# Attention and expert kernel on one core: the order of SyncE's queue at a change of batch

## Chip, cores and metric

The kernel runs on one core of a Trainium2 chip. The metric is the device time of one execution in microseconds (us), smaller is better. A time of the kernel before is the median of three runs.

## The reference, cut to what matters

`x` is 8 x 1024 x 256 (batch, tokens, model), all in float32. A layer norm gives `xn`; attention (16 heads of 64, causal) and a mixture of experts (8 experts, the best 2 of each token, hidden size 1024) both read `xn`, and both are added to `x`:

```python
x = L0_attn_x
xn = _layernorm(x, axis=-1)
# attention
qkv = jnp.einsum('bse,ehd->bshd', xn, w_qkv)
q, k, v = jnp.split(qkv, 3, axis=-1)
out = _attention(q, k, v)                 # causal softmax
a = jnp.einsum('bshd,hde->bse', out, w_out)
# experts: gate[..., None] * y[topi, pos_c], summed over the two choices
x = x + a + _L0_ffn_ref(xn, wg, w1, b1, w2, b2)
```

## The kernel before, in words

Four stages follow one another: layer norm and router, the assignment of tokens to experts, the experts (their results go to `y` in HBM), and then `attention_and_sum`, the longest, in which everything here lies. It computes attention and, beside it, fetches each token's two expert rows and adds them.

**Units.** The attention stage has 64 units: 8 batches (`BATCH`) x 8 pairs of heads (`PAIRS`). Unit `n` belongs to batch `n // 8`, pair `n % 8`. A unit has 20 steps in five rounds of four; each engine walks through the same list of (unit, step), with its own list of what it does at which step. The 1024 queries of a unit are 8 rows of 128, and two rows make a group, 0 to 3. **Group 2 (rows 4 and 5) is the third group, group 3 (rows 6 and 7) the fourth.**

**The probabilities' path.** TensorE computes scores (L1231), VectorE the row minimum (L1355), ScalarE the exponential (L1293), GpSimd scales (L1436). The scaled probabilities must be transposed before TensorE can multiply them by the values (L1263). Groups 0 and 1 are transposed by TensorE. For groups 2 and 3 VectorE transposes 32 x 32 squares (L1398, into `squares`), and then 16 DMAs per group bring each strip of squares to its place in `pT`: 12 of them issued by SyncE in `place` (L1079 to L1085), 4 by GpSimd in `place_rest` (L1460 to L1465). The values product of group 2 of unit `n` runs at step 7 of unit `n + 1`, that of group 3 at step 15 of unit `n + 1`; each waits until all 16 of its strips have landed.

**The result rows.** `res` (128 x 8 x 256 float32, 1 MB, a single buffer) holds the rows of one batch in four groups of 256 KB. It starts as `x` (loaded by `refill`, L1091 to L1094); VectorE adds each pair's output projection to group `g` (L1381, piece `o0` to `o3`), GpSimd adds a tile of expert rows once per unit (`total`, L1500). After the last pair of a batch a group is written out (`store`, L1087 to L1089) and then loaded with the next batch's `x` (`refill` waits for the landing of that group's store, L1093). For unit `n` the pieces `o0` to `o3` belong to unit `n - 1`. So at a change of batch (`n` = 8, 16, ..., 56: seven of them) `store(b-1, 0)` to `store(b-1, 2)` become possible in the middle of unit `n` (VectorE steps 6, 10, 12), but `store(b-1, 3)` only at step 2 of unit `n + 1`. The next batch's `res` is first needed by `total(n)` (GpSimd, step 4 of unit `n + 1`, group 0) and by `o0` to `o3` of unit `n + 1` (VectorE, steps 6, 10, 12 and step 2 of the unit after).

**SyncE's queue** is written out by hand (L1099 to L1125). It is in order: where an instruction waits, all behind it wait. Per unit: the weights `wr` for unit `n + 2` (`load_w`, L1073, two DMAs, once GpSimd has finished with the buffer), one tile of `xn` (L1110), `place(n - 1, 3)`, at a change of batch stores and refills, `place(n, 2)`, and in every second unit the value weights `wvr` (`load_wv`, L1077, two DMAs, once GpSimd is done with the old ones). Before the change, at a change of batch, stores and refills of groups 0 to 2 stand between `place(n - 1, 3)` and `place(n, 2)`, and store and refill of group 3 at the end of the unit, behind `load_wv`. Next in the queue come `load_w`, the `xn` tile and `place(n, 3)` of the following turn of the loop:

```python
if n > 0:
    place(n - 1, 3)
if b > 0 and u == 0:
    for g in range(3):
        store(b - 1, g)
    for g in range(3):
        refill(b, g)
if n < UNITS - 1:
    place(n, 2)
if n % 2 == 0 and n // 2 + 2 < UNITS // 2:
    e.wait_ge(wvlo.sem, wvlo.at(n // 2, MC))
    load_wv(n // 2 + 2)
if b > 0 and u == 0:
    store(b - 1, 3)
    refill(b, 3)
```

Of the kernel before, what the change touches and what calls it, by code (L numbers as in the profile page):

```python
# [845 lines left out]
def attention_and_sum(nc, k, x, xn_dram, w_qkv, w_out, pick, y_dram, out, start):  # L846
# [7 lines left out]
    GROUPS = SEQ // GQ  # L854
# [77 lines left out]
    class Pieces:  # L932
        def __init__(self, sem_, own):
            self.sem, self.value, at = sem_, {}, 0
            for n in range(-1, UNITS + 1):
                for _, p in pieces(n):
                    at += own(p)
                    self.value[n, p] = at
# [5 lines left out]
    with ExitStack() as c:  # L944
# [45 lines left out]
        with ExitStack() as pre:  # L990
# [7 lines left out]
            @block.sync  # L998
            def _(e):
                e.dma_start(wo_raw, wov).then_inc(s_wo, 16)  # L1000
# [63 lines left out]
        def strip(g, a, b):  # L1064

            to, of = slice(b * BL, (b + 1) * BL), slice(a * BL, (a + 1) * BL)
            return wide[g][to, a].rearrange("p x r -> p (x r)"), sq[g][of, b].rearrange("p x k i -> p (x k i)")

        @block.sync
        def _(e):  # L1070
            def load_w(m):
                for c_ in range(MC):
                    e.dma_start(wr[:, 2 * c_:2 * c_ + 2], wv[m % PAIRS][:, c_, :, 0:2 * HDIM]).then_inc(wload.sem, 16)  # L1073

            def load_wv(m):
                for c_ in range(MC):
                    e.dma_start(wvr[:, c_], wvv[m % (PAIRS // 2)][:, c_, :, 2 * HDIM:]).then_inc(wvload.sem, 16)  # L1077

            def place(n, g):  # L1079
                e.wait_ge(squared.sem, squared.at(n, 4 * g - 4))  # L1080
                if n > 0:
                    e.wait_ge(pv.sem, pv.at(n - 1, RUN_OF[g] + 1))
                for a in range(QUARTERS - 1):
                    for b in range(QUARTERS):
                        e.dma_start(*strip(g, a, b)).then_inc(placed[g].sem, 16)  # L1085

            def store(b, g):  # L1087
                e.wait_ge(dve.sem, dve.at((b + 1) * PAIRS, f"o{g}"))
                e.dma_start(outv[:, b, 2 * g:2 * g + 2], res[:, 2 * g:2 * g + 2]).then_inc(stored[g].sem, 16)  # L1089

            def refill(b, g):  # L1091
                if b > 0:
                    e.wait_ge(stored[g].sem, stored[g].at(b - 1, 16))  # L1093
                e.dma_start(res[:, 2 * g:2 * g + 2], xv[:, b, 2 * g:2 * g + 2]).then_inc(rload[g].sem, 16)  # L1094

            e.dma_start(xnt[:], xnv[AHEAD]).then_inc(xload.sem, 16)
            load_w(1)
            load_wv(1)
            for n in range(UNITS):  # L1099
                b, u = n // PAIRS, n % PAIRS  # L1100
                if n == 0:
                    e.wait_ge(s_wolo, 1)
                    for g in range(GROUPS):
                        refill(0, g)
                if n + 2 < UNITS:
                    e.wait_ge(wlo.sem, wlo.at(n, MC))
                    load_w(n + 2)
                if n + 1 + AHEAD < TILES:
                    e.wait_ge(filled.sem, filled.at(n, "xn"))
                    e.dma_start(xnt[:], xnv[n + 1 + AHEAD]).then_inc(xload.sem, 16)  # L1110
                if n > 0:
                    place(n - 1, 3)
                if b > 0 and u == 0:
                    for g in range(3):
                        store(b - 1, g)
                    for g in range(3):
                        refill(b, g)
                if n < UNITS - 1:
                    place(n, 2)
                if n % 2 == 0 and n // 2 + 2 < UNITS // 2:  # L1120
                    e.wait_ge(wvlo.sem, wvlo.at(n // 2, MC))
                    load_wv(n // 2 + 2)
                if b > 0 and u == 0:
                    store(b - 1, 3)
                    refill(b, 3)  # L1125
            for g in range(GROUPS):
                store(BATCH - 1, g)
            for g in range(GROUPS):
                e.wait_ge(stored[g].sem, stored[g].at(BATCH - 1, 16))

        @block.tensor
        def _(e):
# [47 lines left out]
            def turn_p(n, name):  # L1180
                W, unit, at = work_bank(name), min(n, UNITS - 1), 0
                i, h, _, _ = TURNS[name][-1]
                e.wait_ge(scaled.sem, scaled.at(unit, SCALE_ORDER.index((i, h)) + 1))
                for i, h, k0, blocks in TURNS[name]:
                    for b in range(blocks):
                        cols = slice(OFFSET[i] + (k0 + b) * P, OFFSET[i] + (k0 + b + 1) * P)
                        ins = e.transpose(W[:, at * P:(at + 1) * P], room_of(unit, i, h)[:, cols], k["ident"][:])  # L1187
                        at += 1
                return ins

            def work(n, name):

                same = [(m, p) for m in (n - 1, n) if m >= -1 for _, p in pieces(m) if BANK_OF.get(p, 0) == BANK_OF[name]]
                same = same[:same.index((n, name))]
                if same:
                    m, p = same[-1]
                    if by_act(p):
                        e.wait_ge(act.sem, act.at(m, p))
                    if by_dve(p):
                        e.wait_ge(dve.sem, dve.at(m, p))  # L1200
                if name[0] == "p":
                    ins = project(n, name)
                elif name[0] == "v":
                    ins = values_of(n, name)
                elif name == "xn":
                    ins = turn_xn(n)
                elif name[0] == "t":
                    ins = turn_p(n, name)
                else:
                    ins = out_project(n, name)  # L1210
                ins.then_inc(filled.sem, 1)
# [359 lines left out]
```

## Time and profile before

| | |
|---|---|
| median of three runs | 2915.8 us (2915.28 to 2918.36) |
| the profiled execution, its own time | 2915.7 us |
| its span, first to last instruction | 2913.9 us |
| TensorE busy | 2814.5 us, 97% |
| VectorE / ScalarE / GpSimd busy | 2084.7 / 1699.7 / 1723.0 us |
| mean granted TensorE clock | 0.988 |
| mean DMA rate | 128 GB/s; about 150 GB/s in the attention stage |

The profile is of one execution. Its times count from the first instruction; the execution's own time is 1.8 us longer than the span. PE is TensorE, DVE VectorE, ACT ScalarE, POOL GpSimd, SP or SPq SyncE's queue of DMA issues. A line number such as L1085 is that of the kernel's listing. "pT<-squares" is a DMA or a product that writes `pT` from `squares`.

### The profile page before, as it was taken

The numbers are of one execution on the slowest core, as the hardware profiler recorded it, in microseconds if no ns is written. First come the engines' busy times: TensorE is split into PE (matmuls) and PEld (weight loads), VectorE is DVE, ScalarE is ACT, GpSimd is POOL, SyncE is SP. The second block draws the span as 40 slices with busy tenths as digits, with TensorE's granted clock in tenths as the row PEclk, the third lists the DMA queues.
The fourth block names the chain that finished last, engine by engine and source line by source line (L and its number), as shares of the span: only waits on it lengthen the run. The fifth ranks groups of instructions, "written<-read, shape, count | busy, mean of one in ns | idle before, by whom it ended". The sixth has DMA issues, their size and how long they took to land.

```text
span 2913.9 us, 61264 instructions
## 1 busy us (share of the span) xinstructions
PE 2814.5 (97%) x21321; PEld 2284.1 (78%) x21321; DVE 2084.7 (72%) x4448; ACT 1699.7 (58%) x3934; POOL 1723.0 (59%) x2631
## 2 busy tenths in 40 slices
PE   5599999999998999999999999999999999999998
PEld 4489999899997777777777777777777777777776
DVE  7843444344434888888888888888888888888886
ACT  3454444445454666666666666666666666666664
POOL 3032122211212777777877877777777778777774
PEclk9799999999999999999999999999999999999999
DMA  7022212221212565665665565665665556556553
GB/s 241 29 82 75 69 52 83 76 68 47 82 54 74 141 158 144 163 154 145 168 150 145 147 170 147 157 166 142 157 164 151 149 146 176 141 145 183 136 134 93
DMA packets 248774, 371.58 MB, mean 128 GB/s; under 512 B 77392, under 2 KB 177744, under 8 KB 248480
## 3 DMA queue, kind: packets, MB, share of 16 engines
q1 hardware_dynamic: 216000, 276.31, 35.3%
q0 software_dynamic: 32480, 91.44, 11.7%
q8 instruction: 174, 2.85, 0.4%
q14 instruction: 120, 0.98, 0.1%
HBM read 102.80 MB, written 33.55 MB: 47 GB/s over the span
## 4 chain that ended last, share of the span: by engine, by line
PE 66%; DVE 1%; SPq 1%; DMA 0%; issue 0%; ACT 0%; POOL 0%; DVEq 0%; ACTq 0%
PE O L1263 18%; PE S L1231 16%; PE W L1142 12%; PE W L1157 7%; PE W L1176 7%; PE W L1187 6%; SPq L1085 1%; DVE pr L1355 0%; PE W L1165 0%; DMA pT<-squares 0%; DVE squares L1398 0%; ACT pr L1293 0%; DMA out<-res 0%; ACT pT L1283 0%; DVE res L1381 0%
## 5 line engine op out<-in xcount | busy, mean ns | idle before, releaser
L1436 POOL TENSOR_SCALAR pr<-pr,rinv 128x512 f32<-128x512 f32 (+7 forms) x1024 | 748.4, 744 | 399.7 <-DVE rinv L1361 398.6
L1293 ACT ACTIVATE pr<-pr,negm 128x512 f32<-128x512 f32 (+7 forms) x1024 | 787.3, 774 | 285.3 <-DVE negm L1355 285.3
L1355 DVE CUSTOM_DVE_ANT_0 pr<-S,late 128x512 f32<-128x512 f32 (+7 forms) x1024 | 717.0, 751 | 112.9 <-PE S L1231 112.9
L1263 PE MATMUL O<-pT,vv 128*64 128x256 f32 (+1 forms) x5120 | 541.3, 362 | 3.1 <-DMA pT<-squares 3.1
L1398 DVE STREAM_TRANSPOSE squares<-pr 128x640 f32<-128x640 f32 x504 | 494.8, 1020 | 0.0
L1263 PEld LDWEIGHTS O<-pT,vv 128*64 128x64 f32 x5120 | 346.4, 137 | 181.8 <-issue 20.4
L832 DVE TENSOR_TENSOR hl<-h,hh 128x512 fp32r<-128x512 f32 x256 | 192.3, 751 | 315.2 <-ACT hh L793 315.0
L789 ACT ACTIVATE h<-pH,b1c 128x512 f32<-128x512 f32 x256 | 175.9, 687 | 366.0 <-PE pH L719 334.1
L1283 ACT ACTIVATE pT<-W 128x512 f32<-128x512 f32 (+3 forms) x520 | 199.6, 437 | 215.8 <-PE W L1187 215.8
L731 PE MATMUL pY<-w2h,hh 128*128 128x256 f32 x1024 | 287.7, 281 | 2.5 <-DVE hl L832 2.5
L731 PE MATMUL pY<-w2l,hh 128*128 128x256 f32 x1024 | 289.1, 282 | 0.0
L731 PE MATMUL pY<-w2h,hl 128*128 128x256 f32 x1024 | 288.0, 281 | 0.0
L1465 POOL DMA_DIRECT2D pT<-squares x504 | 258.8, 521 | 0.3 <-issue 0.2
L1231 PE MATMUL S<-khf,qh 64*128 64x512 f32 (+2 forms) x1024 | 218.6, 422 | 3.6 <-DVE negm L1355 3.6
L1142 PE MATMUL W<-xnh,wh 128*128 128x512 f32 x512 | 215.1, 420 | 3.0 <-DVE klf L1389 1.5
L719 PE MATMUL pH<-xh,w1h 128*128 128x512 f32 x512 | 205.5, 401 | 4.2 <-DVE xl L804 2.6
L664 POOL COPY idx<-slot_token 128x4 uint32 (+1 forms) x30 | 8.8, 293 | 335.3 <-PE pX L705 335.3
L1142 PE MATMUL W<-xnl,wh 128*128 128x512 f32 x512 | 203.2, 397 | 0.0
L1142 PE MATMUL W<-xnh,wl 128*128 128x512 f32 x512 | 203.1, 397 | 0.0
L719 PE MATMUL pH<-xh,w1l 128*128 128x512 f32 x512 | 201.5, 394 | 0.0
L719 PE MATMUL pH<-xl,w1h 128*128 128x512 f32 x512 | 201.4, 393 | 0.0
L1381 DVE TENSOR_TENSOR res<-W,res 128x512 f32<-128x512 f32 x256 | 175.6, 686 | 35.6 <-PE W L1176 25.4
(176 smaller groups left out, 6479.6 us busy)
## 6 DMA issues: line engine op xcount, KB each, us to landing
pT<-squares SPq DMA_DIRECT2D x756, 128.0 KB
pT<-squares SPq DMA_DIRECT2D x756, 96.0 KB, 2.8
pT<-squares POOLq DMA_DIRECT2D x252, 128.0 KB
pT<-squares POOLq DMA_DIRECT2D x252, 96.0 KB, 3.0
y<-yb SPq DMA_DIRECT2D x128, 128.0 KB, 1.7
wr<-in_L_attn_w_qkv SPq DMA_DIRECT2D x128, 128.0 KB, 2.3
x<-in_L_attn_x SPq DMA_DIRECT2D x16, 512.0 KB, 8.9
xn<-xn SPq DMA_DIRECT2D x16, 512.0 KB, 4.4
```

The lines of the kernel that those rows point to most:

```text
L719: ins = e.matmul(pH[hc % 4][:], w[par][:, m, ws], xx[q][:, m, :], start=(n == 0), stop=(n == 3 * MC - 1))
L731: ins = e.matmul(pY[t % 2][:], hs[q][:, hc, ts_], ws[par][:, hc, :], start=(hc == 0 and n == 0), stop=(hc == HC - 1 and n == 2))
L1142: ins = e.matmul(W, ws[:, 2 * m + of_k], xs[:, t0:t0 + HT, m, :], start=(i == 0), stop=(i == 3 * MC - 1))
L1157: ins = e.matmul(W[:, t * VW:(t + 1) * VW], xs[:, t0 + t, m, :], ws[:, m, :], start=(j == 0), stop=(j == len(terms) - 1))
L1176: ins = e.matmul(W[:, t * MODEL:(t + 1) * MODEL], os_[:, ts_], ws[:, of % PAIRS, :], start=(i == 0), stop=(i == 2))
L1231: ins = e.matmul(S[h][:, off + f * HALF:off + f * HALF + cols], t[hs, i * P:(i + 1) * P], u[f][n % 2][hs, 0:cols], start=(j == 0), stop=(j ...
L1263: ins = e.matmul(O[hs, o0 + a:o0 + GQ], vv[n // 2 % 2][:, kt, vs], turned_p, start=(kt == 0), stop=(kt == KT - 1))
L1293: e.activation(p, p, ACT.Exp, bias=negm[:, c0:c0 + 1], scale=-1.0, accum_out=rsum[:, c0:c0 + 1]).then_inc(expd.sem, 1)
L1355: e.tensor_tensor_reduce(room_of(n, i, h)[:, off:off + w], S[h][:, off:off + w], late[:, SEQ - w:], 1.0, -MASKED, ALU.add, ALU.min, negm[: ...
L1398: e.transpose(sq[g][:, :, 2 * h + i % 2, 0:KT, :], room_of(n, i, h)[:, OFFSET[i]:OFFSET[i] + KT * P].rearrange("p (k b i) -> p b k i", b=Q ...
L1436: e.tensor_scalar(p, p, rinv[:, c0:c0 + 1], 1.0, ALU.mult, ALU.mult).then_inc(scaled.sem, 1)
L1465: e.dma_start(*strip(g, QUARTERS - 1, b)).then_inc(pool_placed[g].sem, 16)
```

## The change

Within the turn of unit `n` at a change of batch, `place(n, 2)` moves ahead of all refills. Store and refill of group 3 move ahead of `load_wv`, and the refills of groups 0 to 2 move behind `place(n, 2)` and behind the store of group 3. The number of DMAs, their sizes and all other engines' programs stay as they are.

```diff
                 if b > 0 and u == 0:
                     for g in range(3):
                         store(b - 1, g)
-                    for g in range(3):
-                        refill(b, g)
                 if n < UNITS - 1:
                     place(n, 2)
+                if b > 0 and u == 0:
+                    store(b - 1, 3)
+                    for g in range(GROUPS):
+                        refill(b, g)
                 if n % 2 == 0 and n // 2 + 2 < UNITS // 2:
                     e.wait_ge(wvlo.sem, wvlo.at(n // 2, MC))
                     load_wv(n // 2 + 2)
-                if b > 0 and u == 0:
-                    store(b - 1, 3)
-                    refill(b, 3)
```

## Rows read from the trace of the kernel before

**Rows 1.** The page's head: busy time by engine.

```profile
PE 2814.5 (97%) x21321; PEld 2284.1 (78%) x21321; DVE 2084.7 (72%) x4448; ACT 1699.7 (58%) x3934; POOL 1723.0 (59%) x2631
```

**Rows 2.** The chain that ended last, its longest pieces: start us, us, what.

```profile
1186.22 3.39 PE O L1263 x32
...
1218.80 3.46 PE O L1263 x32
...
1434.56 3.39 PE O L1263 x32
...
1466.68 3.46 PE O L1263 x32
...
1682.46 3.39 PE O L1263 x32
...
1713.27 3.39 PE O L1263 x32
...
1959.74 3.39 PE O L1263 x32
```

**Rows 3.** The same chain, 1186 to 1225 us, the first change of batch.

```profile
1199.80 4.29 DMA out<-res
...
1206.12 0.51 SPq L1085
...
1213.96 4.79 DMA pT<-squares
```

**Rows 4.** Timeline of SyncE's queue, first change: start us, us, what.

```profile
1185.43 3.49 SPq L1094 DMA_DIRECT2D res<-in_L_attn_x  x3
1189.02 7.59 SPq L1085 DMA_DIRECT2D pT<-squares  x12
1196.65 1.19 SPq L1077 DMA_DIRECT2D wvr<-in_L_attn_w_qkv  x2
1199.80 0.38 SPq L1089 DMA_DIRECT2D out<-res  x1
```

**Rows 5.** The same queue, third change of batch.

```profile
1696.04 0.38 SPq L1089 DMA_DIRECT2D out<-res  x1
1698.25 0.37 SPq L1094 DMA_DIRECT2D res<-in_L_attn_x  x1
...
1700.25 4.01 SPq L1085 DMA_DIRECT2D pT<-squares  x6
```

**Rows 6.** Windows, third change: window, us, PE, PEld, DVE, ACT, POOL, PEclk, DMA share, GB/s.

```profile
1696.10:1697.10 1.00, 1.00 (x12) 0.68 (x10) 1.00 (x2) 1.00 (x4) 0.92 (x3) 1.00 0.14 47
1697.10:1698.00 0.90, 0.90 (x14) 0.77 (x14) 0.90 (x2) 0.72 (x3) 0.90 (x2) 1.00 0.70 239
...
1701.30:1711.30 10.00, 10.00 (x85) 7.86 (x82) 6.80 (x19) 7.23 (x21) 8.28 (x15) 1.00 0.91 254
1711.30:1712.30 1.00, 1.00 (x5) 0.82 (x6) 1.00 (x2) 0.00 (x0) 1.00 (x2) 1.00 0.06 12
```

**Rows 7.** One window, third change: from the store's bytes to the first strips' bytes.

```profile
1697.10:1701.40 4.30, 4.30 (x42) 3.74 (x42) 4.30 (x13) 2.09 (x6) 3.84 (x7) 1.00 0.54 161
```

**Rows 8.** One window ahead of the fourth group's product, fourth change.

```profile
1957.00:1958.00 1.00, 1.00 (x10) 0.69 (x7) 0.99 (x2) 0.00 (x0) 1.00 (x3) 1.00 0.33 90
```

**Rows 9.** First change: the third group's squares (DVE) and its product (PE).

```profile
1186.72 1.83 DVE L1398 STREAM_TRANSPOSE squares<-pr 128x768 f32<-128x768 f32 x2
...
1204.53 1.30 PE L1263 MATMUL O<-pT,vv 128*64 128x256 f32 x10
```

**Rows 10.** First change: GpSimd's total and VectorE's first addition of the new batch.

```profile
1205.00 0.73 POOL L1500 TENSOR_TENSOR res<-res,yg 128x256 f32<-128x256 f32 x1
...
1205.85 0.69 DVE L1381 TENSOR_TENSOR res<-W,res 128x512 f32<-128x512 f32 x1 [0.66 <-POOL res L1500]
```

**Rows 11.** Line L1089, fifth change (2170 to 2180 us): its three stores.

```profile
DMA to landing us min/median/max: 2.3/4.4/4.7
```

**Rows 12.** Line L1094, fifth change (2170 to 2190 us): its three refills.

```profile
DMA to landing us min/median/max: 2.9/4.1/4.9
```

## Prediction

> **What bounds the kernel now.** I read the page's head first: TensorE is busy 97% of the span [rows 1], so only idle stretches of TensorE can be won, and every new one costs. Then the chain that ended last. In the attention stage it runs through TensorE from unit to unit, and the fourth group's product (L1263, x32) marks each unit: 1682.46 to 1713.27 is a unit of 30.81 us [rows 2], and it spans the third change of batch, which costs nothing. The first change does cost: 1186.22 to 1218.80 is 32.58, or 1.8 us too long, and the seven units from there to 1434.56 take 30.82 each, so nothing is regained. The second (1434.56 to 1466.68) is 32.12, 1.3 too long [rows 2]. The eight units from 1713.27 to 1959.74 hold the fourth change and take 30.81 each [rows 2]. In the same way of reading, the three changes after it stall nothing. So two of seven changes stall TensorE, by 3.1 us together. **3.1 us is all that any reordering here could win.**
>
> The chain through the first change says why [rows 3]: from 1199.80 the fourth group's store is under way for 4.29 us, then SyncE issues the refill, the weights and the xn tile, then at 1206.12 the first of twelve strips of `place(n, 3)`; the last is issued at 1213.96 and lands 4.79 us later, and only then the product at 1218.80 starts. What is late is the **fourth** group's strips, and what makes them late is the SyncE queue ahead of them.
>
> **Part 1: the third group's strips start earlier.** In the first change their squares are ready at 1186.72 + 1.83 = 1188.55 [rows 9] and the strips start at 1189.02 [rows 4], 0.47 us late behind the refills. The change takes these 0.47 us away. It is worth nothing: the twelve issues end at 1189.02 + 7.59 = 1196.61, and with a landing as slow as 4.9 us [rows 12] the strips are there at 1201.5, ahead of the product at 1204.53 [rows 9]. Three microseconds of cover hid the old order. Gain: 0.
>
> **Part 2: what now stands ahead of the fourth group's strips.** The moved instructions, each with its queue:
>
> - `store(b-1, 3)` waits for VectorE's addition, not for the queue: SyncE was free at 1196.65 + 1.19 = 1197.84 and idle until 1199.80 [rows 4]. It stays where it is.
> - Three refills go in right behind it. Their wait (stores of groups 0 to 2) is long over, an issue takes 0.37 us [rows 5] and some 0.05 to the next, so 3 x 0.42 = 1.3 us. They lie inside the wait for the fourth store's landing, which is 4.3 us in the first change and 2.2 in the third (1696.04 to 1698.25) [rows 3, 5]. On SyncE's queue: 0.
> - `load_wv`, two DMAs, 1.19 us [rows 4] plus 0.05, used to be issued while SyncE was idle. Now it comes behind the last refill, in the stretch where the chain runs through the queue. That is **1.24 us later for everything behind it**, the two `load_w`, the xn tile and all twelve strips, at all seven changes.
>
> **Part 3: the DMA engines.** The strips are not only late in issue, they are limited by transfer: in the third change the DMA engines are busy 0.91 of 1701.3 to 1711.3, at 254 GB/s [rows 6], until the strips are through. So bytes put ahead of the strips push them. The change puts three refills of 256 KB and `load_wv` with 2 x 128 KB ahead, together 1.05 MB, which at 254 GB/s take 4.1 us. The cheaper price: the fourth group's store of 256 KB kept the engines 0.14 x 1.0 + 0.70 x 0.9 = 0.77 us busy [rows 6], so four such 3.1 us. Against it stands idle time that they can fill: between 1697.1 and 1701.4 the DMA share was 0.54 [rows 7], so 0.46 x 4.3 = 2.0 us. The strips' transfer then moves by 3.1 - 2.0 = 1.1 to 4.1 - 2.0 = 2.1 us, and never by less than the 1.24 of the queue. I take **d = 1.8 us** a change, nearer the upper value, because idle time can't be used to the last bit.
>
> **Part 4: slack.** At the first two changes TensorE already waits for these strips, so d counts in full: 2 x 1.8. At the others there is some slack. In the third the DMA share falls to 0.06 from 1711.3 on [rows 6]; a landing comes about 1 us behind the last bytes (an estimate: of the lone store's 2.2 us some 1.1 pass before its bytes move and 0.9 is the transfer's window), so 1712.3, and the product starts at 1713.27 [rows 2]: 1.0 us of slack. In the fourth the share is still 0.33 between 1957 and 1958 [rows 8] and the product starts at 1959.74: between 0.7 and 1.4. I take 0.9 for the five. They cost 5 x (1.8 - 0.9) = 4.5.
>
> **Part 5: the new rows come later.** Refill 0 used to be issued at 1185.43 [rows 4]; now at about 1200.2, landing 2.9 to 4.9 later by the refills seen [rows 12], so 1203.1 to 1205.1. GpSimd's `total` needs it at 1205.00 and VectorE's addition follows at 1205.85 [rows 10]. At worst 0.1 us late, a little more if the slow first store holds it up, and VectorE waited 0.66 us there anyway without cost to TensorE; I cost it at nothing. If that cover is gone, VectorE's row minima behind the addition come late and TensorE waits for them. Groups 1 to 3 are needed steps later, `load_wv` and `load_w` a unit later or more: nothing.
>
> **The sum.** 0 + 2 x 1.8 + 4.5 = +8.1 us, or 7d - 4.5 in general. The profiled execution took 2915.7, so 2923.8; the median is 2915.8, 0.1 above it, so I say **2924**. Lower bound of the mechanism: d = 1.24 gives 8.7 - 4.5 = +4.2, and with slacks of 1.4 everywhere only the first two count, +2.5. Upper: d = 2.1 with slacks of 0.7 gives 4.2 + 7.0 = +11.2.
>
> **Rival A: the store lands later, so the wait on the path grows (slower still).** In the quiet third change the fourth group's store lands in 2.2 us. Stores with traffic around them took 2.3 to 4.7 [rows 11], refills one behind the other 2.9 to 4.9 [rows 12]. Now three refills are in flight behind the store. If it lands 2.2 us later (4.4, the median of the busy stores), refill 3 and all behind it go by that too: d = 1.24 + 2.2 = 3.4, and 7 x 3.4 - 4.5 = +19.3, 2935. Against it: the store's bytes are ahead of the refills' on the same queue, and the busy stores had strips ahead of them. Chance 0.2. The Trainium skill ("DMA: Bandwidth & Descriptors", section "Latency and other measured facts") gives an HBM access 0.2 us on average and 2 us at high load, and puts most of a DMA's fixed time down to it; by that the landing would take about 4 us and the sum come out near rival A's. The same page ("Queues, rings and completion order") says that a DMA's semaphore waits for the earlier writes of its DMA engine; by that refills behind the store would not hold it. No row before shows a lone store with refills behind it.
>
> **Rival B (not slower): idle time and slack take it all.** The first change loses its slow landing: its store took 4.3 us [rows 3]; with `load_wv` out of the way it might land in 2.2 as in the third change. That brings its strips 4.3 - 2.2 - 1.24 = 0.9 us *earlier*; the second costs 1.24, and the five with d = 1.24 and slack 0.9 cost 5 x 0.34 = 1.7. Sum +2.0, 2917.7. It decides if the first change's store lands in under 3 us and d stays at the queue's 1.24. Against it: `load_wv` was issued 2 us before the store, and little of it can still have been under way. Chance 0.25, together with d at its lower bound alone.
>
> **Rival C: it wins.** The third group's transfers free something on the path. By rows 2 at most 3.1 us can be won. Chance of over 0.2%: 0.03.
>
> **How the numbers follow.** 0.2%, about what a measurement of this kernel can tell from no change, is 5.8 us, which 7d - 4.5 passes at d = 1.47. My forecast (d from 1.4 to 2.4) has 0.52, rival A 0.2, rival B with the low d 0.25, C 0.03. Nearly all of A and nine tenths of the forecast are slower by over 0.2%; the rest of the forecast and B fall within: slower 0.66, same 0.31, faster 0.03. The range reaches from +2 to rival A: 2918 to 2936.
>
> **What would show it.** In the changed kernel's SyncE timeline `pT<-squares` should follow the stores of groups 0 to 2 directly, then out<-res x1, res x3, res x1, wvr x2, wr x2, xnt, pT. The first strip of the fourth group should be issued 4.2 + 1.24 = 5.4 us behind the fourth store at quiet changes (it was 1700.25 - 1696.04 = 4.2 [rows 5]). All seven changes should show a unit over 30.81 us, ended by "DMA pT<-squares" at L1263: about 3.6 and 3.1 too long for the first two, 0.5 to 1.5 for the others. It would be wrong if the wait at L1263 stays at two changes (slack was larger), if the store's wait grows by 2 us (rival A), or if VectorE waits at L1381 for a refill.

## The result and the profile after

| | before | changed |
|---|---|---|
| median (six runs each) | 2915.54 us | 2934.72 us (2931.86 to 2938.81) |
| ratio | | 1.0063, 95% interval 1.0052 to 1.0074 |
| profiled execution: time, span | 2915.7, 2913.9 us | 2933.97, 2932.2 us |

The change makes the kernel 19.2 us slower by the medians (18.3 between the two profiled executions). The ratio is an estimate of its own with its own interval, here and below, and not simply the quotient of the two medians. The page's head and its group for the values product, to set beside [rows 1] (the product is L1262 now, one line up), and the same group in the kernel before:

```profile
PE 2815.5 (96%) x21321; PEld 2281.7 (78%) x21321; DVE 2085.2 (71%) x4448; ACT 1700.0 (58%) x3934; POOL 1727.4 (59%) x2631
...
L1262 PE MATMUL O<-pT,vv 128*64 128x256 f32 (+1 forms) x5120 | 546.7, 365 | 16.8 <-DMA pT<-squares 16.8
```

```profile
L1263 PE MATMUL O<-pT,vv 128*64 128x256 f32 (+1 forms) x5120 | 541.3, 362 | 3.1 <-DMA pT<-squares 3.1
```

TensorE has the same work; its idle time ahead of the values product, ended by a landing strip, was 3.1 us in the kernel before and is 16.8 us. The chain that ended last, its pieces around the first, third and seventh change of batch (start us, us, what; beside [rows 2, 3]):

```profile
1183.55 3.39 PE O L1262 x32
1197.13 4.06 DMA out<-res
1212.04 6.62 DMA pT<-squares
1218.70 5.73 PE O L1262 x32
1251.81 3.39 PE O L1262 x32
...
1685.52 3.39 PE O L1262 x32
1712.33 7.03 DMA pT<-squares
1719.40 3.46 PE O L1262 x32
1750.26 3.39 PE O L1262 x32
...
2680.72 3.39 PE O L1262 x32
2707.20 4.97 DMA pT<-squares
2712.22 3.46 PE O L1262 x32
```

From 1685.52 to 1719.40 is 33.88 us where the kernel before had 30.81 at the same change. (The chain's pieces can begin up to 0.07 us behind the product's first matmul, so sums from the product's own starts, below, differ by that.) The last strip of the first change is issued at 1212.04, 12.66 us behind its squares (11.91 before), but lands 6.62 us later (4.79 before [rows 3]). In the third change it takes 7.03 us. So not only the issue moved; the transfer behind it became slower. Now SyncE's queue at the third change, beside [rows 5]:

```profile
1680.14 4.35 SPq L1089 DMA_DIRECT2D out<-res  x3
1687.89 7.62 SPq L1085 DMA_DIRECT2D pT<-squares  x12
1699.10 0.38 SPq L1089 DMA_DIRECT2D out<-res  x1
1699.52 2.13 SPq L1094 DMA_DIRECT2D res<-in_L_attn_x  x4
1701.69 1.02 SPq L1077 DMA_DIRECT2D wvr<-in_L_attn_w_qkv  x2
1702.76 1.02 SPq L1073 DMA_DIRECT2D wr<-in_L_attn_w_qkv  x2
1703.82 0.47 SPq L1110 DMA_DIRECT2D xnt<-xn  x1
1704.38 7.90 SPq L1085 DMA_DIRECT2D pT<-squares  x11
```

The order is the intended one. From the fourth store to the first strip are 5.28 us, 4.21 before: 1.07 us more, for wvr. The four refills end at 1701.65, 2.55 us behind the store's issue; the store's landing, for which the fourth refill waits, is the same as before:

```profile
DMA to landing us min/median/max: 2.2/2.2/2.2
```

The windows of the third change (DMA share and GB/s in the last two columns) stand against [rows 6, 7]:

```profile
1700.20:1704.50 4.30, 4.30 (x42) 3.72 (x40) 4.29 (x13) 2.09 (x6) 3.85 (x7) 1.00 0.95 290
1704.50:1714.50 10.00, 10.00 (x83) 7.88 (x80) 6.80 (x17) 7.10 (x21) 8.29 (x15) 1.00 1.08 240
1714.50:1718.00 3.50, 1.85 (x10) 1.29 (x9) 3.50 (x7) 2.05 (x6) 1.40 (x2) 1.00 0.80 177
```

The idle time is filled: 0.95 where 0.54 was. But in the ten microseconds behind it the engines move 240 GB/s, where they moved 254 at a share of 0.91. (A share over 1 means that the times of packets overlap on an engine.) This window opens earlier in the strips' course than that of [rows 6]. From the first packet of SyncE's strips to the end of their last one, the changed kernel and the kernel before at the same change, it is

```profile
1706.20:1718.90 12.70, 10.15 (x77) 8.03 (x72) 10.51 (x23) 8.35 (x21) 7.99 (x13) 1.00 0.91 201
```

```profile
1701.60:1711.40 9.80, 9.80 (x83) 7.73 (x79) 6.77 (x17) 6.93 (x21) 8.08 (x15) 1.00 0.91 253
```

The same strips, at the same busy share, take 12.7 us in place of 9.8.

**Where the 18.3 us of the profiled execution are.** By the starts of the fourth group's product, the seven changes are longer by 2.57, 0.96, 3.13, 2.28, 2.43, 1.81 and 0.98, together 14.2 us. The unit behind the first change takes 33.04 instead of 30.80 (+2.2). The last two units and the end take 4.6 us more, and everything up to the first fourth-group product 2.7 less. The last two sums have nothing to do with SyncE's order as far as the trace shows. The unit at +2.2 is TensorE's clock, below, and so are the 4.6: near the end the clock fell to 1.2 GHz three times (at 2882.2, 2899.3 and 2909.5), and in the kernel before not once ahead of the last product.

### The profile page after: what moved, and what is told of

Same layout as the page of the kernel before. It is cut to its first block, busy times and chain, and to the rows that moved or that the text cites. A ratio compares the mean times of both kernels' runs of the same rounds, so it can differ in the third digit from the quotient of the medians.

```text
span 2932.2 us, 61264 instructions
## 1 busy us (share of the span) xinstructions
PE 2815.5 (96%) x21321; PEld 2281.7 (78%) x21321; DVE 2085.2 (71%) x4448; ACT 1700.0 (58%) x3934; POOL 1727.4 (59%) x2631
## 3 DMA queue, kind: packets, MB, share of 16 engines
q0 software_dynamic: 32480, 91.44, 11.7%
## 4 chain that ended last, share of the span: by engine, by line
PE 62%; SPq 2%; DMA 2%; DVE 2%; issue 1%; ACT 0%; POOL 0%; DVEq 0%; ACTq 0%
PE O L1262 17%; PE S L1230 15%; PE W L1141 11%; PE W L1156 7%; PE W L1175 6%; PE W L1186 5%; SPq L1085 2%; DMA pT<-squares 1%; DVE pr L1354 1%; PE W L1164 0%; DVE squares L1397 0%; DMA out<-res 0%; DVE res L1380 0%; ACT pr L1292 0%; SPq L1073 0%
## 5 line engine op out<-in xcount | busy, mean ns | idle before, releaser
L1262 PE MATMUL O<-pT,vv 128*64 128x256 f32 (+1 forms) x5120 | 546.7, 365 | 16.8 <-DMA pT<-squares 16.8
L1262 PEld LDWEIGHTS O<-pT,vv 128*64 128x64 f32 x5120 | 348.8, 138 | 199.1 <-issue 24.3
```

The costliest lines, as they stand in the source:

```text
L1262: ins = e.matmul(O[hs, o0 + a:o0 + GQ], vv[n // 2 % 2][:, kt, vs], turned_p, start=(kt == 0), stop=(kt == KT - 1))
```

## The experiments

"Waits" are TensorE's waits for the fourth group's strips at the seven changes, in a kernel's one profile. The kernel before had a median of 2916.59 us beside experiments 1 to 4, 2914.74 beside 5 to 8 and 2915.82 beside 9 and 10; every ratio is to those same executions.

**1. wvr back at its old place in the changed kernel.**

```diff
-                if b > 0 and u == 0:
-                    store(b - 1, 3)
-                    for g in range(GROUPS):
-                        refill(b, g)
                 if n % 2 == 0 and n // 2 + 2 < UNITS // 2:
                     e.wait_ge(wvlo.sem, wvlo.at(n // 2, MC))
                     load_wv(n // 2 + 2)
+                if b > 0 and u == 0:
+                    store(b - 1, 3)
+                    for g in range(GROUPS):
+                        refill(b, g)
```

> The changed kernel, but the value weights wvr are issued ahead of the fourth group's store, as before the change. That takes 1.2 us of issue and 256 KB out of the stretch between the store and the fourth group's strips; the three refills stay behind the store. Theory (the strips are late by issue time of wvr plus bytes put ahead of them): issue shift 0, three refills of 0.8 to 1.05 us of engine time each against 2.0 us of idle DMA time leave 0.4 to 1.1 us of shift a change; L1262 waits about 2.2 and 1.8 us at the first two changes and under 0.6 at the others; +2 to +6 us over the kernel before (2918 to 2922). Rival (the burst of 1 MB of refills slows the strips whatever is in the queue): half or more of the +18 us stays, 2925 or more. Second rival (only the queue shift counts): 2915 to 2917.

Measured: 2920.13 us, ratio 1.0013 (1.0003 to 1.0023). Waits 1.44, 2.27, 0, 1.08, 0, 0, 0. At the third change SyncE's queue is

```profile
1694.06 0.38 SPq L1089 DMA_DIRECT2D out<-res  x1
1694.49 2.11 SPq L1094 DMA_DIRECT2D res<-in_L_attn_x  x4
1696.64 0.98 SPq L1073 DMA_DIRECT2D wr<-in_L_attn_w_qkv  x2
1697.67 0.47 SPq L1110 DMA_DIRECT2D xnt<-xn  x1
1698.23 3.99 SPq L1085 DMA_DIRECT2D pT<-squares  x6
```

The first strip comes 4.17 us behind the store, as in the kernel before (4.21). With the issue shift gone, the burst of four refills costs 1.7 us of waits in place of 13.7. The time is inside the range of the theory; of the waits, the 1.08 us at the fourth change is above the 0.6 it allowed. So the refills behind the store are mostly absorbed as long as nothing delays the strips' issue.

**2. Only wvr moved, in the kernel before.**

```diff
-                if n % 2 == 0 and n // 2 + 2 < UNITS // 2:
-                    e.wait_ge(wvlo.sem, wvlo.at(n // 2, MC))
-                    load_wv(n // 2 + 2)
                 if b > 0 and u == 0:
                     store(b - 1, 3)
                     refill(b, 3)
+                if n % 2 == 0 and n // 2 + 2 < UNITS // 2:
+                    e.wait_ge(wvlo.sem, wvlo.at(n // 2, MC))
+                    load_wv(n // 2 + 2)
```

> The kernel before, with one thing moved: wvr goes behind the fourth group's store and refill. Refills 0 to 2 stay at their old place. Queue shift 1.24 us in issue at seven changes, 256 KB (1.15 us of engine time by its packets) into 2.0 us of idle DMA time. Theory: first strip issued about 1.1 to 1.2 us later, d = 1.2 to 1.5, +4 to +6 us (2920 to 2922). Rival (refills alone make the loss): under +2 us.

Measured: 2926.54 us, ratio 1.0037 (1.0023 to 1.0051), more than expected.

```profile
L1263 PE MATMUL O<-pT,vv 128*64 128x256 f32 (+1 forms) x5120 | 542.8, 363 | 10.7 <-DMA pT<-squares 10.7
```

Waits 2.29, 1.94, 1.85, 1.49, 1.30, 1.07, 0.75: 7.6 us more than before, from two DMAs in another place. The first strip is 1.1 us later (3.0 instead of 2.0 behind the squares at the third change), and the last one lands 2.9 us later there, and 2.1 on average over the last five changes. An issue shift of 1.1 us became twice as much at the landing: the strips' first packet moved by 1.1 us, and from there to the end of their last packet they took 11.4 us instead of 10.3 (means over these five). The 7.6 us are the larger part of the 13.7 us of added waits, and the miss named what was missing from the theory: the strips themselves go slower.

**3. Third group's strips first, refills 0 to 2 right behind them.**

```diff
-                    for g in range(3):
-                        refill(b, g)
                 if n < UNITS - 1:
                     place(n, 2)
+                if b > 0 and u == 0:
+                    for g in range(3):
+                        refill(b, g)
```

> The third group's strips go first, as in the change, but refills 0 to 2 come right behind them, ahead of wvr, and the fourth group's store and refill stay last. Three refills (1.3 us) and wvr (1.2 us) are then issued where SyncE was idle for 2.0 us, so the fourth store may be 0.5 us late at most. Theory: nothing but a longer landing of the fourth store if the refills' bytes are still under way; 2915 to 2919. Rival (store's landing grows to 4 us with traffic beside it): strips 2 us later at five changes, +8 us or more.

Measured: 2932.29 us, ratio 1.0047 (1.0034 to 1.0061); waits 12.3 us together. The third change:

```profile
1693.24 1.64 SPq L1094 DMA_DIRECT2D res<-in_L_attn_x  x3
1694.92 1.02 SPq L1077 DMA_DIRECT2D wvr<-in_L_attn_w_qkv  x2
1696.76 0.38 SPq L1089 DMA_DIRECT2D out<-res  x1
1700.48 0.37 SPq L1094 DMA_DIRECT2D res<-in_L_attn_x  x1
...
1702.48 1.78 SPq L1085 DMA_DIRECT2D pT<-squares  x3
```

The store is issued on time, 2.25 us ahead of the end of the squares, but lands 3.7 us later instead of 2.2, and refill, weights and strips go with it. The rival expected here is what happened, with 1.5 us in place of 2: with five DMAs close *ahead* of it on its queue the store's landing took 1.5 us longer. Behind it, as in the changed kernel, three refills add nothing.

**4. The fourth group's store and refill behind the fourth group's strips.** In the kernel before:

```diff
                 if n > 0:
                     place(n - 1, 3)
+                if n > PAIRS and u == 1:
+                    store(b - 1, 3)
+                    refill(b, 3)
...
-                if b > 0 and u == 0:
-                    store(b - 1, 3)
-                    refill(b, 3)
```

> The kernel before, with the fourth group's store and refill moved behind the fourth group's strips of the next turn. The wait for the store's landing then stands behind the strips. Theory: the first strip starts 1.6 us behind its squares at all changes as in ordinary units, both waits at L1263 (1.76 and 1.31 us) vanish, 2912.5 to 2913.5 beside 2915.7. Rival (the first two changes are slow for another reason, such as traffic): no gain, 2915 to 2916.

Measured: 2912.47 us, ratio 0.9985 (0.9977 to 0.9994), faster than the kernel before by little, but clear of the noise.

```profile
L1263 PE MATMUL O<-pT,vv 128*64 128x256 f32 (+1 forms) x5120 | 541.3, 362 | 0.0
```

No wait is left. The strips start 1.55 us behind their squares at every change (1.04 at the last), as in the units around them:

```profile
1694.63 8.20 SPq L1085 DMA_DIRECT2D pT<-squares  x12
1702.87 0.58 SPq L1089 DMA_DIRECT2D out<-res  x1
1706.86 0.38 SPq L1094 DMA_DIRECT2D res<-in_L_attn_x  x1
1710.40 1.78 SPq L1085 DMA_DIRECT2D pT<-squares  x3
```

The wait of 4.0 us for the store's landing now stands where SyncE was idle until the next third group at 1710.40.

**5. Do strips of both queues get in each other's way?** By the trace's packet records, from the first strip to the landing of the last, I averaged the packets of 4096 bytes (384 of SyncE's strips and up to 192 of GpSimd's queue) over the third to seventh change. Before: 227 ns (215 to 244 by change). Changed: 276 ns (258 to 289). In the changed kernel the strips of SyncE and GpSimd begin to move within 0.4 us of each other, with the same quarter of the partitions; in the kernel before SyncE's begin 1.8 us ahead. In the changed kernel:

```diff
-                for b in range(QUARTERS):
+                for b in (2, 3, 0, 1):
                     e.dma_start(*strip(g, QUARTERS - 1, b)).then_inc(pool_placed[g].sem, 16)
```

> The changed kernel; GpSimd issues its four strips of a group to the partition quarters in the order 2, 3, 0, 1 instead of 0, 1, 2, 3. In the changed kernel SyncE's and GpSimd's strips begin to move at the same time, both with quarter 0, and their packets of 4096 bytes take 270 to 300 ns, against 215 to 255 at the late changes of the kernel before. Theory P (two strips to the same 32 partitions at once slow each other): the packets fall to under 250 ns at the seven changes, the product's waits shrink by about 1 us each, 2925 to 2929. Rival Q (what slows them is only that two queues are full at the same time): packets stay at 270 to 300 ns and the time at 2931 to 2938.

Measured: 2928.59 us, ratio 1.0046 (1.0032 to 1.0059), beside the changed kernel's 1.0063. Packets took 252 ns, and the waits of the third to seventh change were 0.90, 1.74, 1.46, 1.09 and 1.52, together 6.7 instead of 10.2. The first two waits, 4.58 and 3.97, grew (4.35 and 2.25 in the changed kernel), and the intervals of the two ratios overlap. So what points to theory P are the packets and the waits of one profile, at the five changes where the starts are alike; that the kernel became faster is not shown.

**6. Short refills in the changed kernel.** Refills 0 to 2 of batches 1 to 7 load 32 of 256 columns; the rest of `res` keeps old values, so this kernel leaves out a part of the result.

```diff
-                e.dma_start(res[:, 2 * g:2 * g + 2], xv[:, b, 2 * g:2 * g + 2]).then_inc(rload[g].sem, 16)
+                m = MODEL if b == 0 or g == 3 else MODEL // 8
+                e.dma_start(res[:, 2 * g:2 * g + 2, 0:m], xv[:, b, 2 * g:2 * g + 2, 0:m]).then_inc(rload[g].sem, 16)
```

> The changed kernel; refills 0 to 2 of batches 1 to 7 load only 32 of 256 columns, so the issues stay and seven eighths of their bytes go (this part of the result is left out). The theory (bytes ahead of the strips): what is left is wvr behind the refill, so the waits at the fourth group's product are those of the kernel with wvr last (2.3, 1.9, 1.9, 1.5, 1.3, 1.1, 0.8 us) and the time is near its 2926.5: 2923 to 2928. Rival (the issues and the order count, not the bytes): it stays at 2932 or more.

Measured: 2929.67 us, ratio 1.0042 (1.0028 to 1.0056), a little outside the range.

```profile
L1263 PE MATMUL O<-pT,vv 128*64 128x256 f32 (+1 forms) x5120 | 546.7, 365 | 12.0 <-DMA pT<-squares 12.0
```

12.0 us of waits are near the 10.7 of experiment 2 and below the 16.8 of the changed kernel: the refills' bytes account for some 4.8 us of waits, the place of wvr for most of the rest. The packets still took 278 ns, and the strips 11.4 us from first packet to last, so most of their slowing comes with the later start and not with the refills' bytes.

**7. The changed kernel a second time.**

> The changed kernel once more, for a second profile. If the waits at the fourth group's product are its own, they come out within 1 us of 4.35, 2.25, 3.05, 2.19, 2.34, 1.72, 0.92 (16.8 together). If the falls of the TensorE clock at the first change and in the last two units (2.2 and 4.6 us) depend on chance, they lie elsewhere or are absent, and the total differs by as much.

Measured: 2936.01 us (two runs), ratio 1.0071 (1.0053 to 1.0089). Waits 1.91, 2.45, 2.10, 2.07, 2.73, 3.12, 3.04: 17.4 together, 0.6 from the first profile, but single ones moved by up to 2.4 us, three of the seven by more than the 1 us expected. So a single wait of one profile says little here, while the sum came out alike. Its last two units are those of the kernel before (31.88 us and an end of 30.61), so the 4.6 us lost there in the first profile are not the change's own. What is 2.8 us longer in this profile than in the kernel before, up to the first fourth-group product, was 2.7 shorter in the first: that much varies from one execution to the next.

**8. Both groups' strips first.** Experiment 3 and experiment 4 together.

> The third group's strips ahead of refills 0 to 2 as in the changed kernel, these refills right behind them and ahead of wvr, and the fourth group's store and refill behind the fourth group's strips of the next turn. Theory: no wait at the fourth group's product, since the SyncE queue ahead of it waits for no landing: 2911.5 to 2914, the same as with the third group behind its refills, because the third group's early start is worth nothing. Rival (the third group's start is worth something): over 1 us better than that kernel's 2912.5.

Measured: 2911.0 us, ratio 0.9988 (0.9979 to 0.9997). No wait at the values product. The median is 1.5 us under experiment 4's, but the kernel before was 1.9 us lower beside it too. The interval overlaps that of experiment 4 (0.9977 to 0.9994): the third group's early start is worth nothing that these runs can tell, and costs nothing once no landing stands ahead of the fourth group's strips.

**9. The kernel before, GpSimd's quarters in the order 3, 0, 1, 2.** (The edit is experiment 5's with another order.)

> The kernel before; GpSimd issues its four strips of a group in the quarter order 3, 0, 1, 2. At the changes of batch of the kernel before, SyncE's strips begin to move about three strips ahead of GpSimd's, so with quarter 0 first the two are three quarters apart, and with quarter 3 first they meet in the same one. Theory P (two strips to the same 32 partitions slow each other): 4096-byte packets at the changes from the third to the seventh go from 213 to 246 ns up to 260 or more, their strips land about 1 us later, and small waits appear there, 0 to 1 us each; 2915 to 2919. Rival Q (the fullness of the queues alone): packets stay at 213 to 246 ns and the time at 2915.

Measured: 2917.28 us, ratio 1.0005 (0.9991 to 1.0019). Packets at the third to seventh change took 253 ns instead of 227, the last strips landed 0.6 us later, and one of the five waited, for 0.09 us. Expected were 260 ns and 1 us. The direction is theory P's, the size smaller; no change of the time is shown.

**10. The changed kernel, order 1, 2, 3, 0.**

> The changed kernel; GpSimd's quarter order 1, 2, 3, 0. By theory P the two queues are one quarter apart in place of two: packets of 4096 bytes at the changes from the third on at 235 to 270 ns, clearly under the 275 to 300 of the changed kernel, and the waits there as with order 2, 3, 0, 1 (6.7 us for five) or a little more; 2926 to 2932. Rival Q: as the changed kernel, waits of 10 to 13 us for the five, 2933 or more.

Measured: 2935.73 us, ratio 1.0060 (1.0040 to 1.0081). Packets took 277 ns, waits of the five 11.2 us: as the changed kernel. That speaks against theory P in its simple form; one quarter apart does not help. Experiments 5 and 9 show that the order of GpSimd's four strips alone moves a packet by some 25 ns and a landing by 0.6 to 1 us, but which meetings are slow is **still open**.

The five last changes side by side (means; "start" and "landed" count from the end of the squares, "moving" is from the first packet of SyncE's strips to the end of their last one). SyncE's strips and what moves beside them are 2.5 to 2.6 MB in every kernel:

| kernel | start | landed | moving | 4096-byte packet |
|---|---|---|---|---|
| 8, both groups first | 1.5 us | 13.5 us | 10.3 us | 246 ns |
| 4, fourth store behind | 1.5 | 13.8 | 10.6 | 247 |
| before, 46 units without a change of batch | 1.6 | 13.6 | 10.2 | 253 |
| before | 1.8 | 14.1 | 10.3 | 227 |
| 9, before, other quarter order | 1.8 | 14.7 | 10.8 | 253 |
| 1, refills burst, wvr early | 1.8 | 14.9 | 10.7 | 250 |
| 2, wvr late alone | 2.9 | 16.2 | 11.4 | 272 |
| 6, changed, short refills | 3.0 | 16.5 | 11.4 | 278 |
| 5, changed, order 2, 3, 0, 1 | 3.0 | 16.3 | 10.8 | 252 |
| 10, changed, order 1, 2, 3, 0 | 2.9 | 17.1 | 11.8 | 277 |
| 3, refills ahead of the store | 3.3 | 16.7 | 11.4 | 277 |
| changed; again | 3.0; 3.0 | 17.0; 17.5 | 11.7; 12.3 | 276; 284 |

The packet's time alone does not tell the delay: units that start earliest have packets of 246 to 253 ns and still move their strips in 10.2 to 10.6 us. Slow in these five changes are the groups that start some 3 us behind their squares, within 0.6 us of GpSimd's strips; turned by two quarters (experiment 5) they are not.

## Why the prediction was right, and where it was off

**Direction right, range met by luck.** The kernel became slower, and by the forecast path. 2934.7 lies in 2918 to 2936, but only because the range reached up to rival A, whose mechanism did not occur. The mechanism's own bounds were +2.5 to +11.2, and both the added waits (13.7) and the median (+19.2) lie above them; the point, +8.2 on the median, was under half of what was measured.

**What bounds the kernel: right.** The fourth group's strips behind SyncE's queue. All seven changes now wait there, where two did (by up to 3.1 us at the last five, where 0.5 to 1.5 was expected), and experiment 4 takes away all 3.1 us of waits, the most that reordering could win. The units' starts in its profile give 3.2 us; the medians differ by 4.1, with an interval of 1.7 to 6.7.

**Part 1, the third group's early start is worth 0: right.** Experiment 8 against 4.

**Part 2, the queue: right.** 1.24 us expected, 1.07 to 1.22 measured at the last five changes; the three refills hide in the store's wait (four refills in 2.13 us), and the fourth store is issued when it was.

**Part 3, the transfer: this step failed by its size.** I took d = 1.8 us. By the trace's landings the last strip moved by 2.57, 0.96, 4.14, 2.68, 3.42, 2.45 and 1.69 us, 2.6 on average, outside my 1.1 to 2.1 and also above the 1.4 to 2.4 that the chances used. The idle time was filled as reckoned, 0.54 to 0.95. At the last five changes the landing moved by 2.9 us on average: the strips' first packet by 1.6 (1.1 of issue; of the rest, 0.4 goes with the refills' bytes, since it is gone in experiment 6), and 1.4 more because the strips, with no more bytes beside them, moved in 11.7 us instead of 10.3. That second part stood in the sum at nothing: I took it that the strips' own transfer stays as long as it was. Experiment 2 shows it without the refills: an issue shift of 1.1 us gives 2.1 us at the landing. It is no rule for every change: at the first two, where the strips started late already (4.07 and 2.97 us), the landing moved on average by about as much as the start (1.0 and 0.9 us over the changed kernel, experiment 7 and experiment 2). What slows them is open. The kernel before had already shown the effect, in the landings of its own strips: at its second change they started 1.0 us later behind their squares than at the third (2.97 and 1.96 us) and landed 2.4 us later (16.25 and 13.87). I had priced only the bytes.

**Part 4, slack and the form 7d - 4.5: right.** The slacks were 0.45 to 1.05 us by the landings, 0.8 on average where I took 0.9. With d = 2.6 the form gives +13.7, and the waits at the product grew by 13.7. Two readings were weaker than they looked. My 1 us from the last bytes to the landing does not follow from the lone store (2.2 - 1.1 - 0.9 leaves 0.2); the third change's strips landed at 1712.16, near my 1712.3, by luck. And the fourth change's slack was 0.45, under the 0.7 to 1.4 that I read from the DMA share.

**Part 5, the new rows: right.** In the first change refill 0 landed 4.34 us behind its issue, still 0.45 ahead of GpSimd's total; VectorE waited 0.69 us at its addition, 0.66 before.

**Rival A: its number was met, its mechanism was not.** The store lands in 2.17 us at the five quiet changes although three refills follow it, 2.15 before. With five DMAs close ahead of it (experiment 3) it took 3.5 to 4.4 us, and behind twelve strips (experiment 4) 3.9 to 5.2. The Trainium skill ("DMA: Bandwidth & Descriptors", section "Queues, rings and completion order") says that a DMA's semaphore waits for the earlier writes of its DMA engine. The traces agree: what stands ahead lengthened the landing, and the three refills behind it did not. An estimate from the 2 us that the same page of the Trainium skill gives for an HBM access at high load (section "Latency and other measured facts") was about 4 us; no trace here shows that for DMAs behind the store.

**Rival B: fell.** The first change's store took 4.06 us with wvr out of its way, 4.3 before, and 3.6 in experiment 1, where wvr stands ahead of it again: by these profiles wvr is not what slows it.

**Rival C: fell.** Nothing on the path was won.

**Not in the sum: TensorE's clock.** Some waits were followed by a fall of the granted clock, which made the unit behind longer. That is 2.2 us of the first profile and 1.6 us of the second. The sum did not hold it. The medians' +19.2 exceeds the waits' 13.7 by more than one such fall. Falls near the end, worth 4.6 us in one of the changed kernel's two profiles and nothing in the other, differ from execution to execution; how much of the medians' difference they make is not shown.

## What to carry to other kernels

On an in-order DMA queue, look for what stands ahead of the transfer that the bounding engine waits for; put waits for a landing (store, then refill) behind it, at a place where the queue idles. Time added to the issue of a group of transfers that keeps the DMA engines full can be much less than its delay (1.1 us became 2.1 to 2.9 at five of seven changes here), since it can also change what the group meets on its way. Moving a small load out of an idle stretch of the queue into the path cost here more than three refills of three times its bytes.

## What the runs showed of the hardware

**Overlapping SBUF-to-SBUF transfers.** Where SyncE's strips began to move 1.5 to 2.5 us ahead of GpSimd's, 4096-byte packets took 227 to 253 ns on average and the strips were through in 10.2 to 10.8 us. Where both began within 0.6 us, it was 272 to 284 ns and 11.4 to 12.3 us, and with the quarters turned by two (experiment 5) 252 ns and 10.8 us.

**TensorE's clock after a wait.** The first change in two windows (PEclk is the third column from the right), and the 14 us behind them:

```profile
1215.00:1219.00 4.00, 0.30 (x2) 0.29 (x4) 2.33 (x4) 2.13 (x6) 2.04 (x4) 0.69 0.72 165
1219.00:1226.00 7.00, 7.00 (x45) 4.03 (x41) 0.42 (x1) 0.39 (x1) 3.65 (x6) 0.69 0.72 193
1226.00:1240.00 14.00, 14.00 (x115) 11.41 (x115) 13.81 (x31) 9.12 (x22) 7.46 (x12) 1.00 0.14 38
```

TensorE had waited 4.35 us; the clock stood at 1.2 GHz from 1216.5 to 1223.3, and the product took 5.73 us in place of 3.46. But the relation is loose. Over the ten profiles with waits, falls followed waits of 1.94 to 4.58 us at fifteen places, and thirteen waits between 1.94 and 3.12 us had none. A fall made the unit behind 1.4 to 2.7 us longer. In experiment 10 there were five of them in one profile, with a span of 2939.9 us. So a wait can cost half as much again as its own length, or more, and whether it does differs from one execution to the next.

In the last units of a kernel, where TensorE has gaps anyway, the clock fell in seven of the twelve profiles and not in the others. The changed kernel's first profile and its second, in the same stretch of the program (it lies 6.2 us later in the second):

```profile
2880.00:2890.00 10.00, 8.22 (x61) 5.98 (x62) 6.41 (x17) 4.01 (x11) 8.68 (x15) 0.83 0.75 180
```

```profile
2886.20:2896.20 10.00, 7.82 (x68) 6.00 (x68) 7.64 (x23) 5.60 (x15) 8.67 (x15) 1.00 0.75 178
```

Why it falls in the one and not in the other was not tried.
